# Causal attention with two passes of scores: TensorE's second-pass scores move one position ahead, and the next batch's preparation moves to other positions

## The reference, cut to what matters

```
def adaptive_temperature_softmax(logits):
    p = softmax(logits)
    entropy = sum(-p * log(p + 1e-09), axis=-1)
    beta = where(entropy > 0.5, maximum(poly(entropy), 1.0), 1.0)
    return softmax(logits * beta)

q, k, v = (proj(W) for W in (Wq, Wk, Wv))       # x is layer-normalised first
sim = einsum('bhid,bhjd->bhij', q, k) / sqrt(8)
sim = where(causal, neg, sim)
out = einsum('bhij,bhjd->bhid', adaptive_temperature_softmax(sim), v)
x = x + out_reshaped @ Wo.T + bo
```

## Time and profile before

| | us |
|---|---|
| median of 3 executions (lowest, highest) | 2694.11 (2691.54, 2702.1) |
| the profiled execution, its own time | 2696.02 |
| its span in the trace | 2694.2 |
| the attention's first unit read by ACT | at 1006.46 |
| its last `exp2` of the stage starts | at 2174.5 |

### The profile page before, as it was taken

How to read it: one execution, slowest core, us unless ns; L and a number is a source line. 1 busy time by engine, 2 the same in 40 slices (tenths; PEclk the granted TensorE clock), 3 DMA queues, 4 the chain that set the end, 5 groups by cost and what they waited for, 6 DMA issues and landing times. The chain is left out here.

```text
span 2694.2 us, 23532 instructions
## 1 busy us (share of the span) xinstructions
PE 1694.7 (63%) x6573; PEld 748.6 (28%) x6573; DVE 1548.0 (57%) x3577; ACT 1393.0 (52%) x2650; POOL 73.8 (3%) x71
## 2 busy tenths in 40 slices
PE   3544554899999944477777787677877642122172
PEld 2222332344444420122223222232222210111141
DVE  3444343445353449987788777977777134477411
ACT  2222222434343319888988999898989531000020
POOL 0000000000000010000000000000000000000314
PEclk9666666999999975566667656776667875555586
DMA  3000000555555510110101010201010100100212
GB/s 119 0 0 0 0 0 0 137 152 133 145 141 144 153 51 25 35 70 21 59 19 75 19 60 18 84 18 56 23 55 7 43 3 12 24 0 0 91 62 74
DMA packets 55812, 143.38 MB, mean 53 GB/s; under 512 B 7640, under 2 KB 22648, under 8 KB 53088
## 3 DMA queue, kind: packets, MB, share of 16 engines
q1 hardware_dynamic: 53648, 137.84, 17.3%
q0 software_dynamic: 2048, 4.20, 0.5%
HBM read 124.56 MB, written 17.45 MB: 53 GB/s over the span
## 5 line engine op out<-in xcount | busy, mean ns | idle before, releaser
L1273 DVE CUSTOM_DVE_ANT_0 sa_lg<-sa_e,sa_lg 128x1024 f32<-128x1024 f32 (+7 forms) x512 | 387.0, 756 | 162.6 <-ACT sa_lg L1185 162.6
L1053 PE MATMUL sa_ps<-sa_k1s,sa_q1s 72*128 72x512 bf16 (+3 forms) x768 | 297.2, 456 | 233.6 <-DVE sa_nmax L1264 197.0
L1175 ACT ACTIVATE sa_e<-sa_e,sa_nmax 128x1024 f32<-128x1024 f32 (+7 forms) x512 | 401.3, 784 | 48.6 <-DVE sa_nmax L1264 48.3
L1264 DVE CUSTOM_DVE_ANT_0 sa_e<-sa_ps,sa_mask 128x1024 f32<-128x1024 f32 (+7 forms) x512 | 385.3, 753 | 36.6 <-PE sa_ps L1053 34.9
L1185 ACT ACTIVATE sa_lg<-sa_e,sa_sum 128x1024 f32<-128x1024 f32 (+7 forms) x512 | 400.6, 782 | 2.7 <-DVE sa_prod L1273 2.2
L1193 ACT ACTIVATE sa_p<-sa_ps 128x512 f32<-128x512 f32 x576 | 336.5, 601 | 110.1 <-PE sa_ps L1087 55.8
L1084 PE MATMUL sa_ps<-sa_q2s,sa_k2s 75*128 75x512 bf16 (+3 forms) x768 | 299.9, 428 | 91.7 <-ACT sa_p L1193 70.1
L701 DVE TENSOR_TENSOR mx_hw<-mx_spread,mx_h 128x512 f32<-128x512 f32 x256 | 176.3, 691 | 252.2 <-ACT mx_h L608 242.5
L608 ACT ACTIVATE mx_h<-mx_ps 128x512 f32<-128x512 f32 (+1 forms) x264 | 156.7, 596 | 286.0 <-PE mx_ps L544 277.7
L544 PE MATMUL mx_ps<-mx_f,m 128*128 128x512 f32 x512 | 263.0, 595 | 1.7 <-ACT mx_h L608 1.7
L557 PE MATMUL mx_ps<-mx_hw,m 128*128 128x512 f32 x512 | 262.0, 594 | 1.7 <-DVE mx_hw L701 1.7
(11 more groups left out here) (287 smaller groups left out, 1952.4 us busy)
## 6 DMA issues: line engine op xcount, KB each, us to landing
mx_spread<-mx_spill SPq DMA_DIRECT2D x256, 256.0 KB, 4.0
sa_q1s<-sa_spill_q SPq DMA_DIRECT2D x96, 96.0 KB
sa_k1s<-sa_spill_k SPq DMA_DIRECT2D x96, 96.0 KB
sa_q2s<-sa_spill_q SPq DMA_DIRECT2D x48, 192.0 KB
sa_k2s<-sa_spill_k SPq DMA_DIRECT2D x48, 192.0 KB
m<-m_in SPq DMA_DIRECT2D x1, 4256.0 KB, 16.0
be_w<-w_in SPq DMA_DIRECT2D x16, 256.0 KB, 6.1
sa_spill_q<-sa_qp SPq DMA_DIRECT2D x4, 768.0 KB, 13.3
```

Source lines behind the costliest of these rows:

```text
L1053: last = nc.tensor.matmul(out[:, col:col + w], q_ring[:, c % 2, local, i * P:(i + 1) * P], k_ring[:, c % 2, local, col:col + w], start=Tru ...
L1175: nc.scalar.activation(e[:, u % 5, 0:w], e[:, u % 5, 0:w], ACT.Exp, scale=-1.0, bias=nmax[:, b % 2, i, h:h + 1], accum_out=sums[:, b % 2, ...
L1264: nc.vector.tensor_tensor_reduce(out=e[:, u % 5, 0:w], in0=slot_of("unit", u)[:, 0:w], in1=mask_wide[:, SEQ - w:SEQ], scale=1.0, scalar=3. ...
L1273: nc.vector.tensor_tensor_reduce(out=lg[:, u % 2, 0:w], in0=e[:, u % 5, 0:w], in1=lg[:, u % 2, 0:w], scale=1.0, scalar=0.0, op0=ALU.mult, ...
```

## The change

PE's order within a position becomes: `score(u + 2)`, the pieces of position u + 1 with their answers, then the turning work. The pieces stand one position ahead and in front of the turning work.

The preparation of the next batch moves from positions 75 to 90 to positions 13 to 53: the layer norm to 13, 14, 16, 17, 18 and 20, `fill_a` and `take_a` from 83 to 23, the query's projection from 86 to 33, the key's from 88 to 44. The steps of the two splits are dealt out, one instruction at every second position. The writes of q and k to DRAM move from positions 92 and 97 to 43 and 53. The scaled query gets a scratch tile of its own. The value projection stays where it is, and no computation is added or left out.

```diff
+        left2 = sb("sa_left2", [P, SEQ])
...
-        A_AT, Q_AT, K_AT, V_AT = 83, 86, 88, 106
+        A_AT, Q_AT, K_AT, V_AT = 23, 33, 44, 106
...
-                    if (b := batch_at(u, 92)) is not None:
+                    if (b := batch_at(u, 43)) is not None:
                         spill_first("q", b, q_split, q_parts, spill_q, q_spilled)
-                    if (b := batch_at(u, 97)) is not None:
+                    if (b := batch_at(u, 53)) is not None:
                         spill_first("k", b, k_split, k_parts, spill_k, k_spilled)
...
                     if u + AHEAD < ALL1:
                         score(u + AHEAD)
+                    for m in pieces2_at(u + 1):
+                        second(m)
+                        if m % GROUP == GROUP - 1 and m >= GROUP:
+                            answer(m // GROUP - 1)
+                    if group_at(u, 2) == ALL_GROUPS - 1:
+                        answer(ALL2 - 1)
                     if (k := side_at(u, WIDE_AT)) is not None:
                         widen(k)
...
                         out_project(b)
-                    for m in pieces2_at(u):
-                        second(m)
-                        if m % GROUP == GROUP - 1 and m >= GROUP:
-                            answer(m // GROUP - 1)
-                    if group_at(u, 2) == ALL_GROUPS - 1:
-                        answer(ALL2 - 1)
...
-                    if (b := batch_at(u, 77)) is not None:
+                    if (b := batch_at(u, 16)) is not None:
                         ln.square(nc, act, b, 1)
-                    if (b := batch_at(u, 79)) is not None:
+                    if (b := batch_at(u, 18)) is not None:
                         ln.root(nc, act, b, 1, load=False)
...
-                    split_up(q_cm[k // 2 % 2][rows, :], left[rows, :], parts_of(q2_parts, rows), q2_split, steps)
+                    split_up(q_cm[k // 2 % 2][rows, :], left2[rows, :], parts_of(q2_parts, rows), q2_split, steps)
...
-                    if (b := batch_at(u, 75)) is not None:
+                    if (b := batch_at(u, 13)) is not None:
                         ln.total(nc, seq(b))
-                    if (b := batch_at(u, 76)) is not None:
+                    if (b := batch_at(u, 14)) is not None:
                         ln.subtract(nc, dve, b, 1, seq(b))
-                    if (b := batch_at(u, 78)) is not None:
+                    if (b := batch_at(u, 17)) is not None:
                         ln.variance(nc, dve, b, 1)
-                    if (b := batch_at(u, 80)) is not None:
+                    if (b := batch_at(u, 20)) is not None:
                         ln.scale(nc, dve, b, 1, y_tm[:, :, :])
...
                         take_q(b)
-                        split_q(b, range(0, 3))
-                    if (b := batch_at(u, Q_AT + 1)) is not None:
-                        split_q(b, range(3, 5))
+                    for r in range(5):
+                        if (b := batch_at(u, Q_AT + 1 + 2 * r)) is not None:
+                            split_q(b, range(r, r + 1))
                     if (b := batch_at(u, K_AT)) is not None:
                         take_k(b)
-                    if (b := batch_at(u, K_AT + 1)) is not None:
-                        split_k(range(2, 4))
-                    if (b := batch_at(u, K_AT + 2)) is not None:
-                        split_k(range(4, 5))
+                    for r in range(2, 5):
+                        if batch_at(u, K_AT + 2 * r) is not None:
+                            split_k(range(r, r + 1))
```

## The result

The changed kernel takes 2711.17 us (median of 7 executions, 2708.11 to 2719.25) against 2697.47 us for the kernel before in the same session (7 executions, 2691.54 to 2703.12). The ratio is 1.0054, with a 95% interval of 1.0036 to 1.0072: 14.6 us slower by the ratio (the interval is 9.7 to 19.4 us) and 13.7 us by the medians. No change had been forecast, at 2690 us, with a gain of 3.7 us in the sum. The time lies inside the wide range of 2660 to 2718, but above the forecast's own range, which ended at 2707. That the kernel got slower is clear of noise; whether it is by more than the 13.5 us that were called no change is not.

The account below looks back on a forecast made before the run. ACT was taken to bound the two-pass stretch, with DVE's preparation and the DMA transfer ending each cycle. +23.7 - 7.9 - 10.6 + 1 - 2.5 gave a 3.7 us gain: 2690 us, own range 2681 to 2707, 8-in-10 range 2660 to 2718.

Parts of the forecast that it names:

- part 1: PE's new order: about +1 us over seven cycles, and a loss of 2.5 us in the tail.
- (a): Preparation chain, entropy to last cast: 1 us shorter though `widen` comes 1.7 us later; ACT's 4.96 us wait shrinks to about 1.
- (b): Group start: PE reaches the DMA wait one position earlier, a score behind it; loss 0.3 us a cycle, bounds 0 and 1.
- (c): Double position with an answer between, one per group: loss 0.5 us a cycle.
- (d): Tail: the last side's pieces and answer come in front of `widen`; loss 2.5 us, bounds 0 and 4.
- Parts 2 and 3: Preparation leaves the second side, gain 23.7 us, and arrives in the first side, loss 7.9 us.
- Part 4: Batch 1's preparation moves into the first pass alone: first side 18.3 us later, next cycle 7.7 us less; loss 10.6 us.
- A: Rival: ACT's gaps, 71.5 us of waits on PE, close; faster, 2667 us; chance 0.22.
- B: Rival: the first side hides more of the moved preparation; faster, 2678 us; chance 0.15.
- D: Rival: preparation costs 13 us in cycles one and three in place of 3.8; slower, 2710 us; chance 0.07.
- C: Rival: scores come too late behind a piece and an answer; 29 us slower, 2720 us; chance 0.13.

Follow-up runs that it names:

- turn_later: The changed kernel with turn_answers and DVE's normalising at position 10 of the next group in place of 8; 2690.6 us, 0.9962 of the kernel before.
- turn_front: The changed kernel with turn_answers still at position 8 but issued in front of that position's pieces and answer; 2688.99 us, 0.9967 of the kernel before.
- order_turn10: The kernel before with PE's new order, the old preparation, and the turn of the answers at position 10 in place of 8; 2697.43 us, 0.9995.
- front_only: The kernel before with the pieces of position u itself moved in front of the turning work, not one position ahead; 2702.01 us, 1.0007.
- order_only: The kernel before with PE's new order alone, the preparation left at positions 75 to 90; 2724.05 us, 1.0081.
- ahead_only: The kernel before with the pieces computed one position ahead but still behind the turning work; 2702.78 us, 1.0000.
- old_turn10: The kernel before with one edit: answers turned and normalised at position 10 in place of 8; 2714.32 us, 1.0051.
- prep_only: The kernel before with the moved preparation alone (positions 13 to 53), PE's old order kept; 2702.11 us, 1.0012.
- keys_early: The kernel before with the key half of each even group's reload issued before its side ends; 2686.23 us, 0.9944.
- all_new: The changed kernel with the turn at position 10, batch 1's preparation at its old late positions, and the early key reload; 2661.43 us, 0.9866.
- both: The kernel before with preparation moved for batches 2 and 3 only, plus the early key reload, in PE's old order; 2676.01 us, 0.9919.

## Why the prediction was wrong

**The step that failed** is the sum of part 1: "Sum: (1 - 0.3 - 0.5) for each of seven cycles is about +1, so a cycle stays as it is." It followed three things that the pieces now stand in front of, `widen`, the score at the group's start and the score behind an answer. It left out `turn_answers`, though it was on the list of work that the order passes. Nothing in the trace of before shows a wait there, but the rows to price it were at hand: a piece and an answer of 0.61 + 1.91 us in front of it, at a position where DVE has 0.6 us of room. The runs show 3 us of DVE's standing, twice a cycle, and about 3 us a cycle on the time: 20 us between the changed kernel and `turn_later` or 22 us to `turn_front` (23 to 25 by the ratios). With this item out of the way the forecast gain was a little too small: `turn_later` is 10 us faster than the kernel before (interval 6 to 15), where 3.7 were forecast.

**(a)** was right in kind and near in size. `widened` waits 2.01 us for `widen` in place of 1.33, and the chain is 24.1 us in place of 25.4. ACT's 4.96 us at `widen` are gone, and 3.2 us of them came back at once as its wait for the turned shifts (19.9 us in six), which the prediction didn't have.

**(b) and (c)** can be read where the turn does no harm: from the kernel before to `order_turn10` the ratio is 0.9995. The new order by itself is worth nothing, and (1 - 0.3 - 0.5) a cycle was a fair price for all but the turn. Its clean cycles show both sides of the sum: the preparation chain is 24.4, 22.4 and 23.9 us for 25.0, 24.4 and 25.0 before, and from the new group's first piece to the next entropy it takes 90.1, 89.8 and 90.1 us for 89.0, 88.7 and 89.0.

**(d)** was right: in the tail the preparation chain went from 12.9 to 15.8 us, 2.9 us longer, where 2.5 were forecast, and `widen` came later behind the pieces and answers. `front_only`, which puts pieces in front of `widen` and has almost no stall at the turn (3.6 us in all from 1150 to 2083), shows it apart. DVE's `widened` after the last side, in the kernel before, in the changed one and in `front_only`:
```profile
2090.71 1.23 DVE L1311 TENSOR_TENSOR sa_q<-sa_ps,sa_q 64x1024 f32<-64x1024 f32 x1 [2.14 <-PE sa_ps L1061]
2111.68 1.23 DVE L1312 TENSOR_TENSOR sa_q<-sa_ps,sa_q 64x1024 f32<-64x1024 f32 x1 [5.07 <-PE sa_ps L1062]
2091.69 1.23 DVE L1311 TENSOR_TENSOR sa_q<-sa_ps,sa_q 64x1024 f32<-64x1024 f32 x1 [6.36 <-PE sa_ps L1061]
```
The chain of `front_only` is 17.1 us, 4.2 more than before. What the prediction did not have is that this price hangs on the granted clock. From entropy to `widened`, `front_only` and then `turn_later` (columns as in the earlier trace rows):
```profile
2080.50:2091.69 11.19, 10.64 (x40) 4.23 (x40) 4.28 (x19) 4.25 (x9) 0.00 (x0) 0.51 0.01 1
```
```profile
2080.46:2086.23 5.77, 5.20 (x38) 2.39 (x31) 4.28 (x20) 3.33 (x7) 0.00 (x0) 1.00 0.00 0
```
At the low level (0.50 to 0.56, near 1.2 GHz) the chain is 12.9 us before, and 15.8 us in the changed kernel, 15.9 in `order_only` and 17.1 in `front_only` and `ahead_only`. At 1.00 (2.4 GHz) it is 11.2 us in `old_turn10`, which has the old order, 11.7 in `turn_later` and 12.9 in `turn_front`. So the size of 2.5 us came true in part by luck. Another 4.32 us of the changed kernel's tail is DVE standing for the turn ahead of the last entropy (the row at 2099.58 in its order of time); it lies outside the chain and belongs to the step that failed.

**Parts 2 and 3** hold as a pattern, and their sizes hold once the turn is out of the way: the cycles of `turn_later` against the forecast are 140.5 and 139.1 for 139.7 (one and three, columns 2 and 4 of the table), 136.2 and 137.3 for 137.2 (two and four, columns 3 and 5). With the old order they were off. `prep_only` has 142.5 and 141.2, 138.6 and 139.0, 7.5 us more than forecast in the four. The four of `turn_front` (138.8, 139.4 and 139.0, 136.0) add up to the forecast within 0.6 us, though one of them is 1.8 off. There ACT's wait for pieces remains (39.2 + 32.0 us), and in `turn_later` it is 26.2. That the pieces computed ahead cover the projections was assumed by the prediction; it is argued from these sums, not shown apart.

**Part 4** was right: 18.1 us for 18.3, and its cycle 138.8 in the changed kernel and 136.7 in `turn_later` for 136.7.

**The rivals.** A did not come. ACT's wait for pieces in the long stretch fell from 71.5 to 34.5 us, and in `order_turn10` to 14.0 us, with no gain in time: there it waits 30.0 us for DVE's maxima and 17.8 us for the turned shifts instead, where it waited 6.2 us and nothing. The Trainium skill (Perfetto Trace Analysis, Identifying the Most-Contended Engine) has one optimise the engine with the highest occupancy first. ACT is that engine here, but the runs do not bear out that its waits for PE were the prize: what was taken from them came back in its other waits, and a cycle's end hangs on a chain through DVE and the DMA. B did not come: the first side cost what was forecast. D asked for waits of 3 us and more at the projections; DVE's longest wait for one is 1.8 us, in the long stretch. C named 2720 us, scores too late behind an answer, to be seen by DVE's waits for L1053. They rose as it said, 19.9 to 108.3 us, and `ahead_only` shows that they cost nothing in sum. It was the right family, something behind an answer, and the wrong member. The transfer's price was taken from rows, 80 GB/s, and `keys_early` measured it apart: 0.59 MB in 7.1 us is 83 GB/s. The Trainium skill (DMA: Bandwidth & Descriptors, Bandwidth) gives 6.15 us for 1 MB loaded over 128 partitions by DMAs that GpSimd issues, by which half of the reload would be an estimated 3.6 us. The reload here goes to 24 rows at a time and is issued by SyncE; its measured time is twice that estimate, and decides.

**What stays open**: with the turn mended, the new order is worth 1 us with the old preparation (`order_turn10`), 12 us with the moved one (`turn_later` against `prep_only`) and 15 us in `all_new` against `both`. That the moved preparation is what it hides fits these three, but no run takes a single projection apart. How much of the 20 us is the turn's stall itself and how much the lower granted clock that goes with it is open too. Open too is how much of the 9 us by which the two traces differ beyond the medians is spread from execution to execution.

## What to carry to other kernels

When a block of work moves forward in an engine's list, write down every item that it passes, one by one with its consumer, and price each, even where the trace of before shows no wait: the one left out cost 20 us here. Run an interaction of two halves as a square, since two edits that each cost nothing cost 22 us together, and moving a third item two positions on gained 20 us in the one order and cost 14 us in the other. A large new wait (DVE's 143 us for scores) may be free, and a small one (35 us in twelve) may be the loss; what tells is whether the waiting engine has room until its consumer needs it.

## What the runs showed of the hardware

The same turn of eight matmuls took 1.97 us in the changed kernel (at 1327.14) and 1.10 us in `turn_later` (at 1325.01). The granted clock of the two stretches tells them apart (columns as in the earlier trace rows), first the changed kernel, then `turn_later`:
```profile
1325.30:1329.10 3.80, 3.80 (x27) 2.35 (x26) 0.88 (x4) 3.54 (x7) 0.00 (x0) 0.50 0.19 78
```
```profile
1325.00:1326.10 1.10, 1.10 (x10) 0.98 (x9) 1.10 (x3) 1.10 (x5) 0.00 (x0) 0.94 0.19 78
```
At 0.50 (1.2 GHz) answer and turn are 3.9 us in a row, at nearly full clock (2.4 GHz) the turn alone is a little over half as long as at the low level. So a 3 us stall would be shorter at the high level. But the low level alone doesn't make the stall. In `turn_front` the turn at 1320.70 took 1.92 us at the same 0.50, and DVE did not stand for it:
```profile
1320.70:1322.60 1.90, 1.90 (x10) 1.65 (x8) 1.90 (x6) 1.90 (x6) 0.00 (x0) 0.50 0.19 82
```
Over the long stretch the clock was 0.62 in the changed kernel and 0.66 in `turn_later`, though both programs have the same instructions. The mean clock is not by itself the cause of the loss: `ahead_only` had 0.63 at the time of before, and `old_turn10` had 0.67 and was 14 us slower.
